# A branch of TensorE's hand-written loop moves in front of the propagation product

## What is computed

```python
z = sigmoid([x_t, h] @ Wz + bz)
r = sigmoid([x_t, h] @ Wr + br)
h_cand = tanh([x_t, r * h] @ Wh + bh)
h_new = (1 - z) * h + z * h_cand
h_next = where(prop, tanh(h_new @ Wp + bp), h_new)   # prop: every 4th step but the last
```

## Time and profile before

| what | value |
|---|---|
| time, median of 3 runs | 7794.21 us (7791.9 to 7794.97) |
| span of the profiled execution | 7788.3 us |
| mean granted TensorE clock | 0.992 |
| TensorE busy, matmuls | 7651.5 us, 98% |
| TensorE busy, weight loads | 7376.8 us, 95% |
| VectorE, ScalarE, GpSimd busy | 74%, 59%, 24% |
| packets on the instruction queue q8 | 45 (0.74 MB) |

### The profile page before, as it was taken

The page is one execution under the profiler, slowest core; times in us unless marked ns, Lnnn a source line. Parts: engine busy times, 40 slices in busy tenths (PEclk is TensorE's granted clock), DMA queues, the critical chain, the costliest instruction groups (busy, mean ns, idle before and its releaser), DMA issues.

```text
span 7788.3 us, 1085382 instructions
## 1 busy us (share of the span) xinstructions
PE 7651.5 (98%) x492632; PEld 7376.8 (95%) x492632; DVE 5745.9 (74%) x31679; ACT 4597.4 (59%) x27263; POOL 1837.6 (24%) x8079
## 2 busy tenths in 40 slices
PE   5999999999999999999999999999999999999997
PEld 4999999999999999999999999999999999999997
DVE  3777777777777777777777777777777777777776
ACT  2666666666666566666666666666666666666654
POOL 2222222222222222222222222222222222222220
PEclk7999999999999999999999999999999999999999
DMA  2000000000000000000000000000000000000000
GB/s 73 12 12 12 14 12 11 13 12 12 11 14 12 12 13 13 12 11 14 11 12 12 14 12 11 14 11 12 11 14 12 11 13 12 12 11 14 11 11 7
DMA packets 153809, 105.25 MB, mean 14 GB/s; under 512 B 19072, under 2 KB 152576, under 8 KB 152576
## 3 DMA queue, kind: packets, MB, share of 16 engines
q1 hardware_dynamic: 153728, 104.22, 4.4%
HBM read 62.20 MB, written 41.94 MB: 13 GB/s over the span
## 4 chain that ended last, share of the span: by engine, by line
PE 98%; DVE 1%; issue 1%; POOL 0%; ACT 0%; DMA 0%; SPq 0%; POOLq 0%; DVEq 0%
PE ps_r L512 24%; PE ps_c L512 23%; PE ps_l L501 19%; PE ps_z L501 18%; PE ps_mid L479 8%; PE ps_p L490 6%; DVE ps_c L741 0%; DVE l_T L737 0%; PE ps_mid L565 0%; POOL l_state L410 0%; POOL l_state L406 0%; ACT l_state L910 0%; DVE l_pre L786 0%; DMA rnn_h<-w_rnn_h 0%; DVE scan_add L850 0%
## 5 line engine op out<-in xcount | busy, mean ns | idle before, releaser
L512 PE MATMUL ps_c<-c_h,rh 128*2 128x64 f32 x131072 | 2219.3, 219 | 10.0 <-issue 10.0
L512 PEld LDWEIGHTS ps_c<-c_h,rh 128*2 128x2 f32 x131072 | 1888.5, 84 | 11.6 <-issue 11.6
L501 PE MATMUL ps_l<-rnn_h_parts,l_state 128*6 128x128 bf16 x98304 | 1829.9, 220 | 65.7 <-POOL l_state L410 65.2
L966 ACT ACTIVATE r_tanh<-ps_r 128x4 f32<-128x4 f32 x4096 | 710.9, 174 | 1628.2 <-DVE ps_r L741 1552.3
L501 PEld LDWEIGHTS ps_l<-rnn_h_parts,l_state 128*6 128x6 bf16 x98304 | 1536.7, 86 | 101.6 <-ACT ps_l L877 69.9
L741 DVE STREAM_TRANSPOSE ps_r<-ps_r 128x64 f32<-128x64 f32 x4096 | 1087.7, 266 | 403.4 <-PE ps_r L512 303.0
L741 DVE STREAM_TRANSPOSE ps_c<-ps_c 128x64 f32<-128x64 f32 x4096 | 1075.0, 262 | 110.2 <-PE ps_c L512 12.5
L512 PE MATMUL ps_r<-r_h,h_odd 128*2 128x64 f32 x65536 | 1136.8, 219 | 16.5 <-DVE h_odd L858 6.0
L512 PE MATMUL ps_r<-r_h,h_even 128*2 128x64 f32 x65536 | 1103.4, 219 | 14.6 <-DVE h_even L858 11.7
L406 POOL TENSOR_TENSOR l_state<-l_state 128x8 f32<-128x8 f32 x2048 | 415.5, 203 | 2877.2 <-ACT l_state L910 2877.2
L512 PEld LDWEIGHTS ps_r<-r_h,h_odd 128*2 128x2 f32 x65536 | 969.2, 85 | 85.6 <-DVE h_odd L858 33.9
(11 more groups left out here) (110 smaller groups left out, 10311.0 us busy)
## 6 DMA issues: line engine op xcount, KB each, us to landing
gates_spill<-gates_rows SPq DMA_DIRECT2D x128, 192.0 KB, 2.0
gates_seeds<-gates_spill SPq DMA_DIRECT2D x768, 16.0 KB
x_next<-xT SPq DMA_DIRECT2D x128, 64.0 KB, 1.8
x_mid<-xT SPq DMA_DIRECT2D x128, 64.0 KB, 1.8
rnn_spill<-rnn_rows SPq DMA_DIRECT2D x128, 64.0 KB, 1.6
rnn_seeds<-rnn_spill SPq DMA_DIRECT2D x512, 16.0 KB
gates_seeds<-gates_spill SPq DMA_DIRECT2D x512, 8.0 KB
gates_seeds<-gates_spill SPq DMA_DIRECT2D x256, 32.0 KB
```

The costliest lines, as they stand in the source:

```text
L501: last = nc.tensor.matmul(psum[QUAD * j:QUAD * j + PARTS * B, 0:P], state_parts(k), w_parts[:, k, j, q, :], start=False, stop=(k == KT - 1 ...
L512: last = nc.tensor.matmul(pair[QUAD * j:QUAD * j + B, n, at:at + W], stationary(k), w[:, k, P * j + W * n:P * j + W * (n + 1)], start=Fals ...
L966: nc.scalar.activation(r_tanh[:, k, :], r_T[n][:, :, 0:B], ACT.Tanh, scale=0.5).then_inc(r_tanh_done[n], 1)
```

## The change

The first of the two branches behind the propagation, the one between early and late, moves in front of it. Since the branch leaves the body "group", the propagation has to stand in both bodies to which it leads:

```diff
                 with arm("group"):
-                    propagation(groups)
                     pe.br_lt(even, after_mid, on_true=label("early"), on_false=label("late"))
                 with arm("early"):
+                    propagation(groups)
                     pe.br_lt(even, after_logits, on_true=label("logits"), on_false=label("mid"))
...
                 with arm("late"):
+                    propagation(groups)
                     pe.br_lt(even, after_gates, on_true=label("gates"), on_false=label("last"))
```

## The result

The changed kernel takes 7808.95 us (median of 16 runs, 7798.03 to 7815.35), the kernel before 7796.98 us (16 runs, 7791.9 to 7800.61). The ratio is 1.0016, 95% interval 1.0009 to 1.0023: slower by 7 to 18 us. The two profiled executions have spans of 7796.2 and 7788.3 us, 7.9 us apart.

The account below looks back on a forecast made before the run. TensorE, 98% of the span, was taken as the bound, limited at group ends by a data chain or its sequencer. Terms 0.08 + 0.09 - 0.05 + 0.04 = +0.16 us a chunk, 126 times: +20 us, 7814 us; range 7795 to 7826.

Parts of the forecast that it names:

- front: Before the propagation's first load: later start by 0.08 us at logits, 0.01 mid, 0.27 gates, 0.08 last.
- behind, to ps_r: From propagation to ps_r: saved 0.04 us at logits, 0.06 at mid, 0.18 at gates, nothing at last.
- steps: From ps_r's first load to the next group end: taken as unchanged, 0 in all four arms.
- The needs: From L671's start to the propagation's first load: 0.25 us in early arms (logits, mid), 0.39 in late (gates, last).
- the 0.18 us of idle: Behind the propagation at gates: TensorE idle put down to issue, to come back nearly whole, -0.18 us.
- they fill the wait, they don't set it: At last: projection loads end at 3022.67, inside the data chain's 1.74 us wait for ps_r; nothing saved behind.
- faster: Rival: front branch hides everywhere behind the wait for h_pre; only savings count, -35 us, 7759; chance 0.09.
- No change: Rival: front branch cheaper than those measured behind the propagation, step not paid twice or jump half; 7795 to 7804, chance 0.20.
- a step of 0.06 us: Between two adjacent branches: sequencer time belonging to neither, 0.06 us, counted in the front cost.
- Dearer: Rival: fetch traffic strikes between L671 and propagation, 0.1 us more at two group ends, +25 us, about 7840; chance 0.08.
- Code that no longer stays in the core: Rival: TensorE's loop, grown by 64 instructions, is fetched anew each chunk, +155 us, 7949; chance 0.03.

Follow-up runs that it names:

- the fetches released by z: Gate-input fetches released by the ps_z product instead of ps_r, some 0.7 us later: kernel before 7713.59 us, changed kernel 7719.29 us.
- the unused copy: Kernel before plus a second propagation between mid and late that is never run, branches as before: 7791.16 us against 7791.10, ratio 0.9999.

## Why the prediction was right

The forecast was 7814 us, or +20, for the reason named: the front branch is paid where the sequencer has no lead. Measured are +12.0 us (7 to 18). The direction and the mechanism came as forecast; the size lies at the low end of the stated range, and a chunk loses 58 ns in the trace where the working had 160. Point by point, in ns:

```
                     front                       behind, to ps_r            steps
               logits mid gates last       logits  mid gates last   logits mid gates last
predicted         80   10   270   80         -40  -60  -180    0        0    0    0    0
measured          96   29   270   92         -41  -66  -126   -1      -45  -77  -32  -42
```

- The front cost was right in each arm. The needs come out as 255 and 396 ns from L671 to the load, where 0.25 and 0.39 us had been added up from single branches, steps and issue. That a jump costs three times a fall was tested by turning the direction round, and the role of lead by taking the traffic away: with it gone, logits and mid pay nothing.
- Behind the propagation three of four terms were right, counted by loads. At gates the 0.18 us of idle were to come back whole, and 126 ns did. The idle went to 0.01 us, but the 32 loads of the projection then took 1.62 us to the next ps_r (3009.57 to 3011.19) instead of 1.54 (3006.61 to 3008.15 in the kernel before). The matmuls show why: the loads had stood still for 0.18 us, the matmuls for less. From the propagation's first matmul to the projection's it was 0.97 us before and is 0.87 now (gates), and 1.05 and 0.93 at mid (time line of TensorE's matmuls; first the kernel before, then the changed one):

```profile
3005.67 1.06 PE L490 MATMUL ps_p<-prop_w,h_pre 128*2 128x128 f32 x32
3006.64 1.93 PE L479 MATMUL ps_mid<-rcz_x,x_new 128*32 128x256 f32 x32
...
2990.96 1.10 PE L490 MATMUL ps_p<-prop_w,h_pre 128*2 128x128 f32 x32
2992.01 1.08 PE L479 MATMUL ps_mid<-ih,x 128*32 128x128 f32 x32
```

```profile
3008.81 1.06 PE L490 MATMUL ps_p<-prop_w,h_pre 128*2 128x128 f32 x32
3009.68 1.91 PE L479 MATMUL ps_mid<-rcz_x,x_new 128*32 128x256 f32 x32
...
2993.91 1.09 PE L490 MATMUL ps_p<-prop_w,h_pre 128*2 128x128 f32 x32
2994.84 1.08 PE L479 MATMUL ps_mid<-ih,x 128*32 128x128 f32 x32
```

- The step that failed is what the prediction says of the projection's loads, "they fill the wait, they don't set it", from which the prediction took the time behind ps_r's first load as unchanged. By loads the steps get 196 ns shorter, a term that it had at nothing. Most of that is the same saving behind the propagation, seen late: the first load of ps_r may come when the new state is there, while its first matmul comes behind the projection's matmuls, which run later than their loads. Worked out from the same traces, the mean way from the propagation's first matmul to the first of ps_r goes from 1871, 1907, 2718 and 1781 ns (logits, mid, gates, last) to 1807, 1777, 2599 and 1746. That is 348 ns a chunk behind the propagation where 280 were forecast, 130 of them at mid (forecast 60) and 35 at last (forecast 0). At last the propagation and the projection now take 873 and 874 ns, within 4 ns of the least that any kernel here shows, so no idle between their matmuls is left. In the steps 74 ns remain, whose cause stays open. With the fetches released by z, the change gives back 140 ns behind the propagation and 37 in the steps.
- Added up by matmuls, in ns a chunk: front 479 (forecast 440), behind -348 (-280), steps -74 (0), together 57 instead of 160. The front was forecast 39 too cheap; the other two terms, 142 together, made the forecast too high.
- The rival "faster" failed at the place named for it: the lead is 307 at last and 121 at gates, and 397 are needed. "No change" was to come from a step of 0.06 us not paid twice; it is paid, 255 in the early arms being about 69 + 77 for the two branches and 110 for the step to the second one and the way from it to the load. "Dearer" wanted 0.1 us more in front at two group ends; no front is more than 20 ns above its term.
- Code that no longer stays in the core: the instruction queue q8 has 46 packets instead of 45, and between 210 and 7530 us a single one. The Trainium skill (Runtime: NRT & Kernel Launch, Instruction fetch mechanics) gives TensorE room for 2,048 instructions; the trace agrees that the grown loop is held, and the unused copy costs nothing. The Trainium skill (Advanced Engine Details and Errata, Control Flow Timing) has one price of 108 ns for a compare-and-branch; the runs show two, 64 to 83 and 201 to 216. The prediction says that its sum would come to about nothing by that price; taken through its own steps the price gives an estimate of 0.05 to 0.13 us a chunk, 6 to 16 us, but nearly nothing in front at last (0 to 0.03 us), where 92 ns were measured.

```profile
q1 hardware_dynamic: 143636, 88.74, 4.0%
q14 instruction: 10, 0.08, 0.0%
q8 instruction: 1, 0.02, 0.0%
```

## What to carry to other kernels

A branch costs what its time, and the step behind it, exceed the lead that the sequencer has over its engine at that place; read the lead from the start of the branch to the first instruction behind it, at each place, before a branch is moved. A wait for data hides a branch only if the sequencer reaches the branch early enough, and a stall in front is partly given back behind: in most pairs of kernels here the sum of stalls was more than the loss. Where loads run ahead of matmuls, count an engine's idle time at the matmuls before calling it a gain. When a lead is missing at some turns of a loop and not at others, look for what else runs at those turns: here the gain lay in the release of a transfer, in another engine's program, and was six times what the branches were worth.

## What was not expected of the hardware

The fetches of the gate inputs, DMA traffic of 12 to 24 GB/s, slow the stream of TensorE's loads: 1.10 us instead of 0.87 from ps_c to ps_l, and no lead left at L671 in many group ends, where the load comes 115 ns after the start of a branch of 69. The runs show that it is these fetches (the lead comes back at the ends from which they are taken away, twice, by an earlier and by a later release). It is not the amount of traffic. In the kernel before, ps_l of the first step behind gates runs with no DMA beside it, and that behind logits while the gates are written out at 266 GB/s; each window goes from the first matmul of ps_l to the first of the next product, and both are 0.70 us long (busy and count for each engine, clock, DMA share, GB/s):

```profile
3010.82:3011.52 0.70, 0.70 (x63) 0.69 (x51) 0.65 (x4) 0.54 (x5) 0.00 (x0) 1.00 0.00 0
3039.76:3040.46 0.70, 0.70 (x63) 0.69 (x51) 0.65 (x4) 0.54 (x5) 0.25 (x1) 1.00 0.74 266
```

What it is in the fetches that slows the loads stays open. And where the same bytes fall decides 180 us of 7790: 7892.69 with the release 4.2 us earlier, 7791.25 as it was, 7713.59 with it 0.7 us later.
